# q and k projected transposed and stacked block-diagonally by DMA, four heads scored per whole-array product, in a fused attention and mixture-of-experts block

## What is computed

```python
# x [16, 256, 128]; 16 heads of 8; cos, sin [256, 4]
h = layernorm(x) * (1 + ca) + sa                 # ca, sa, ga ... per batch, from c
q, k, v = h @ WQ.T + bq, h @ WK.T + bk, h @ WV.T + bv
q, k = rope(q), rope(k)       # halves of a head: x1*cos - x2*sin, x1*sin + x2*cos
scores = einsum('bhqd,bhkd->bhqk', q, k) / sqrt(8)
attn = softmax(where(causal, scores, -inf))
x = x + ga * ((attn @ v) @ Wo.T + bo)
h = layernorm(x) * (1 + cb) + sb
x = x + gb * moe(h)           # 8 experts of 512 hidden, top 2 of 8 by the router
```

## Time and profile before

| what | value |
|---|---|
| median of 3 runs | 774.05 us (770.82 to 779.35) |
| the profiled execution | 777.98 us |
| its span, first to last instruction | 776.2 us |
| PE busy | 610.2 us (79%) |
| DVE busy | 443.2 us (57%) |
| ACT busy | 364.6 us (47%) |
| POOL busy | 355.9 us (46%) |
| mean granted TensorE clock | 0.719 |

### The profile page before, as it was taken

One profiled execution on the slowest core, in us unless ns is written; L12 is line 12 of the kernel. 1 busy time (PEld: TensorE's weight loads), 2 busy tenths in 40 slices (PEclk: granted clock), 3 DMA queues, 4 the chain that ended last, 5 costly groups with the idle time before them and its releaser, 6 DMA issues.

```text
span 776.2 us, 15198 instructions
## 1 busy us (share of the span) xinstructions
PE 610.2 (79%) x4224; PEld 450.2 (58%) x4224; DVE 443.2 (57%) x1882; ACT 364.6 (47%) x1003; POOL 355.9 (46%) x515
## 2 busy tenths in 40 slices
PE   1589898898899889888986667586698787899960
PEld 1355665565655555656554444354488677798960
DVE  2367657647465585575696838270356644467753
ACT  0234553553544535545433434243376655677740
POOL 2223344343242442442523665645335477755552
PEclk9755866755655666666565858565599999999985
DMA  3833199000000000000000000100112122233433
GB/s 100 268 114 125 42 130 126 15 8 8 7 7 14 7 7 14 5 9 7 7 15 4 26 31 18 32 18 27 28 36 55 46 74 69 73 83 99 141 87 118
DMA packets 48560, 40.70 MB, mean 52 GB/s; under 512 B 6347, under 2 KB 44756, under 8 KB 48257
## 3 DMA queue, kind: packets, MB, share of 16 engines
q1 hardware_dynamic: 43968, 31.68, 18.6%
q0 software_dynamic: 4544, 8.47, 3.3%
HBM read 24.35 MB, written 16.69 MB: 53 GB/s over the span
## 4 chain that ended last, share of the span: by engine, by line
PE 54%; DVE 15%; POOL 10%; issue 9%; DMA 7%; ACT 3%; DVEq 1%; SPq 1%; POOLq 0%; ACTq 0%
PE ps_pv L1327 9%; PE misc L1270 8%; PE ps_sc L1310 5%; PE misc L1378 5%; PE ps_max L1292 5%; DVE ps_max L1074 4%; POOL sorted_rows L537 4%; PE ps_sc L1218 4%; PE misc L1349 3%; DMA results<-qkv,probs 3%; PE ps_max L1225 2%; DMA probs<-sorted_rows 2%; PE ps_max L1294 2%; POOL probs L575 2%; PE ps_pv L1225 2%
## 5 line engine op out<-in xcount | busy, mean ns | idle before, releaser
L1074 DVE CUSTOM_DVE_ANT_0 ps_max<-ps_max,mask_q 128x128 f32<-128x128 f32 (+1 forms) x512 | 166.4, 389 | 79.2 <-PE ps_max L1294 79.0
L743 ACT ACTIVATE probs<-ps_sc 128x384 f32<-128x384 f32 x256 | 121.8, 490 | 184.3 <-PE ps_sc L1312 183.1
L575 POOL TENSOR_SCALAR_AFFINE_SELECT probs<-probs 128x512 f32<-128x512 f32 x128 | 81.8, 641 | 167.5 <-ACT probs L743 167.4
L1327 PE MATMUL ps_pv<-probs,v_wides 128*32 128x256 f32 (+1 forms) x1024 | 87.1, 483 | 29.5 <-POOL probs L575 29.4
L546 POOL DMA_INDIRECT results<-qkv,probs x78 | 79.3, 1017 | 67.6 <-DVE qkv L891 54.3
L1310 PE MATMUL ps_sc<-qm_stack,k_stacks 26*128 26x256 f32 x256 | 104.0, 480 | 2.5 <-ACT probs L743 2.5
L702 ACT ACTIVATE early_a<-ps_sc,v_wides 128x128 f32<-128x128 f32 x312 | 98.4, 373 | 3.2 <-PE ps_sc L1218 2.7
L1218 PE MATMUL ps_sc<-x_in,v_wides 128*128 128x128 f32 x624 | 87.3, 285 | 6.9 <-DVE probs L883 6.6
L1218 PEld LDWEIGHTS ps_sc<-x_in,v_wides 128*128 128x128 f32 x624 | 78.1, 197 | 10.1 <-issue 9.6
L1292 PEld LDWEIGHTS ps_max<-k_stacks,q_stack 24*128 24x128 f32 x256 | 39.0, 239 | 67.1 <-DVE maxima L1074 41.3
L1327 PEld LDWEIGHTS ps_pv<-probs,v_wides 128*32 128x32 f32 x1024 | 35.7, 147 | 68.0 <-POOL probs L575 29.4
(11 more groups left out here) (135 smaller groups left out, 1034.5 us busy)
## 6 DMA issues: line engine op xcount, KB each, us to landing
sorted_rows<-blank_s SPq DMA_DIRECT2D x1, 5070.0 KB, 42.5
probs<-sorted_rows SPq DMA_DIRECT2D x78, 65.0 KB, 1.9
gates<-gate_rows SPq DMA_DIRECT2D x1, 4096.0 KB, 12.5
x_in<-in_x SPq DMA_DIRECT2D x16, 128.0 KB, 2.1
x_res<-in_x SPq DMA_DIRECT2D x16, 128.0 KB, 2.1
wfc_s<-in_w_fc SPq DMA_DIRECT2D x1, 2048.0 KB, 9.3
wproj_s<-in_w_proj SPq DMA_DIRECT2D x1, 2048.0 KB, 8.8
heads_ts<-results SPq DMA_DIRECT2D x8, 256.0 KB, 3.1
```

The source lines that it names most:

```text
L575: nc.gpsimd.affine_select(two, two, [[0, 2], [0, 2], [1, P]], ALU.is_ge, 0.0, base=0, channel_multiplier=-1).then_inc(S["causal_done"], 1)
L743: nc.scalar.activation(probs[:, h % 8, :], ps_sc[h % 2][:, 0:384], ACT.Exp, scale=SCALE).then_inc(S["exp_done"], 1)
L1074: last = nc.vector.tensor_tensor_reduce(ps_max[h % 3][:, a * P:a * P + n], ps_max[h % 3][:, a * P:a * P + n], mask_q[:, T - n:T], 1.0, MASKED,
L1327: last = nc.tensor.matmul(ps_pv[rows, a * P:T], vw[:, a, h, :], probs[:, h % 8, :].rearrange("p (c q) -> p c q", q=P)[:, a:3:2, :], start= ...
```

## The change

A step now has 12 slots (units), three to each group of four heads: units 0 and 1 hold two heads each with queries 0 to 255 against keys 0 to 127, unit 2 holds four heads with the later queries against the later keys. A unit is 512 columns. t starts at -2.

- The weights' columns are permuted once. q and k of batch t+1 are projected transposed (`qk`, two products of 256 columns), and once more with the halves of each head exchanged (`rot`, two more); v has its own two products of 128 columns. DVE adds bias and multiplies by the cosine or sine in one instruction (4 per step), POOL sums 512 columns, ACT writes the high part, DVE the low part (one of 512 columns each), and v's bias (`values`).
- SP stacks the parts: 26 DMAs from SBUF to SBUF per step (`stack_rows`), k block-diagonally in a tensor that is zero elsewhere. It waits for the low part of batch t+1 and for the last scores of batch t-1.
- First pass: one whole-array product of 512 columns per unit, and a second product (identity by mask, both bf16) of 512 or 256 columns that adds the mask. DVE takes plain maxima, one TENSOR_REDUCE of 512 per unit.
- Shifts: per group of four heads DVE writes 16 columns (2 instructions), PE transposes them (`sh0` to `sh3`), ACT copies, SP writes them with 4 DMAs into the rows of q (`shift_rows`).
- Second pass: 2 or 4 whole-array products per unit. Unit u is scored in slot u + 7, that is from slot 7 of step t to slot 6 of step t+1 (`LAG = 7`). exp takes 512 columns, 12 times a step.
- Heads are turned back in slot 10 of step t+1, one step sooner. The gates come by one DMA per step; one for the end of the kernel is a broadcast of 2 MB in step 3, ahead of the blanking.

```diff
+UNITS = 3 * GROUPS
+LAG = 7
-    for t in range(-1, FIRST):
+    for t in range(-2, FIRST):
 USES = {
...
+    0: [('zT', 1), ('attnT', -2)],
+    1: [('sh3', -1), ('qk', 1)],
+    2: [('rot', 1)],
+    3: [('wo', -2)],
+    4: [('sh0', 0)],
+    7: [('sh1', 0), ('z2T', -2)],
+    9: [('router', -2), ('v', 1)],
+    10: [('sh2', 0), ('heads0', -1), ('heads1', -1)],
 }
+PV_AT = {11: (0, 0), 2: (1, -1), 5: (2, -1), 8: (3, -1)}
+SHIFT_AT = {2: 0, 5: 1, 8: 2, 11: 3}
+def exp_unit(n):
+    return ((n - LAG) % UNITS, -1 if n < LAG else 0)
...
+                def shift_rows(g, d):
+                    if s.has(d):
+                        s.wait(sp, S["shift_out"], d, 4, g + 1)
+                        for part in range(2):
+                            for a in range(TILES):
+                                at = (a * 2 + part) * 4
+                                sp.dma_start(part_rows(q_stack[(s.t + d) % 2], part)[:, g, a * P:(a + 1) * P],
+                                             shift_t[g % 2][at:at + 4, :].bitcast(F32)).then_inc(S["shift_in"], 16)
+                def stack_rows():
+                    if not s.has(1):
+                        return
+                    s.hold(sp, S["low_done"], 1, 1, 1, S["sp_passed"])
+                    s.hold(sp, S["score_mm"], -1, UNITS, UNITS, S["sp_passed"])
+                    n = (s.t + 1) % 2
+                    for w in range(4):
+                        for j, part in enumerate((high, low, high)):
...
+                            sp.dma_start(k_diag[n][at:at + DK, :, w, :].bitcast(F32), part[ROWS * w:ROWS * (w + 1), 1, :].bitcast(F32)).then_inc(S["stacked"], 16)
+                        for j, part in enumerate((high, high, low)):
...
+                    for part in range(2):
+                        sp.dma_start(part_rows(q_stack[n], part), zero_row[:].bitcast(F32).rearrange("p (o t) -> p o t", o=1).broadcast_to([4, GROUPS, T])
+                                     ).then_inc(S["stacked"], 16)
+                shift_rows(3, -1)
+                shift_rows(0, 0)
+                stack_rows()
+                shift_rows(1, 0)
+                shift_rows(2, 0)
...
                 if s.t == 3:
+                    sp.dma_start(gates[:], gate_dram[:, D:2 * D].rearrange("(o b) d -> o b d", o=1).broadcast_to([P, B, D])
+                                 ).then_inc(S["gate_in"], 16)
...
+                for n in range(UNITS):
...
+                    if s.has(0):
+                        maxima_of(n)
+                        if n in SHIFT_AT:
+                            shift(SHIFT_AT[n])
+                    if n == 2 and s.has(1):
+                        turn_with("qk", turned_a, 0, "qk_turned")
+                    if n == 3 and s.has(1):
+                        turn_with("rot", turned_b, 2, "rot_turned")
                     if n == RESIDUAL_AT and s.has(-2):
                         residual()
...
+                    if n == 6 and s.has(1):
+                        low_part()
...
+                def scores(u, d):
+                    g, c = divmod(u, 3)
+                    if c == 0:
+                        s.wait(pe, S["shift_in"], d, 4 * SHIFTED, SHIFTED * (g + 1))
...
+                    u, d = exp_unit(n)
+                    if s.has(d):
+                        scores(u, d)
+                    if n in PV_AT and s.has(PV_AT[n][1]):
+                        weigh(*PV_AT[n])
+                    for name, d in USES.get(n, []):
                         if s.has(d):
-                            fill(name)
+                            fill(name, d)
                     if s.has(0):
-                        for m in MAX_AT.get(h, ()):
-                            scores_for_max(m)
+                        scores_for_max(n)
```

More of the change, by code:

```diff
@@ L246, in block_program @@
         gate_row = sb("gate_row", [B, 4 * D])
-        gates = sb("gates", [P, B, 4 * D])
+        gate_now = [sb(f"gate_now{n}", [P, 4 * D]) for n in range(2)]
+        gates = sb("gates", [P, B, D])
         x_in = [sb(f"x_in{n}", [P, TILES, D]) for n in range(2)]
@@ L1047, in divide @@
+                    s.wait(dve, S["attn_tr"], -2, 1, 1)
                     nc.vector.tensor_tensor(attn[:, a], m[:, :, 0:DK],
@@ new lines, in shift @@
+                def shift(g):
+                    s.wait(dve, S["max_done"], 0, UNITS, 3 * g + 3)
+                    if g >= 2:
+                        s.hold(dve, S["shift_tr"], 0, 4, g - 1, S["dve_passed"])
+                    else:
+                        s.hold(dve, S["shift_tr"], -1, 4, g + 3, S["dve_passed"])
+                    if s.t == 0 and g == 0:
+                        dve.wait_ge(S["zeroed"], 8)
+                    m = maxima[:, :, 4 * g:4 * g + 4]
+                    v = shifts[:, g % 2, 0:16].rearrange("p (a f w) -> p a f w", a=TILES, f=2)
+                    nc.vector.tensor_scalar(v[:, :, 0], m, -1.0, None, ALU.mult).then_inc(S["shift_high"], 1)
+                    s.wait(dve, S["shift_high"], 0, 4, g + 1)
+                    nc.vector.scalar_tensor_tensor(out=v[:, :, 1], in0=m, scalar=-1.0, in1=v[:, :, 0].bitcast(F32),
+                                                   op0=ALU.mult, op1=ALU.subtract).then_inc(S["shifts_done"], 1)
@@ L1117, in emit @@
+                    if n == 8 and s.has(2):
+                        s.slot_wait(dve, x_loaded, 2)
+                        statistics(s, 2, x_in[s.t % 2], stats, moments, "stats_done", "moments_done")
+                    if s.t == LAST and 4 * n < GROUP_TILES[0]:
+                        if n == 0:
                             dve.wait_ge(S["loaded_w"], 48)
                             dve.wait_ge(S["logits_done"], GROUP_B[0])
-                        find_top(range(3 * h, min(3 * h + 3, GROUP_TILES[0])))
@@ L1144, in _ @@
+                    if n == 9 and s.has(1):
+                        values()
+                    if n == 10 and s.has(2):
+                        normalise(s, 2, x_in[s.t % 2], moments, rstd, z, "rstd_done", "z_done", "zt_done")
+                    if n == UNITS - 1 and s.has(-1):
+                        divide(0)
+                        divide(1)
             steps(dve, emit)
@@ L1315, in weigh, with shift_turned @@
+                def shift_turned(g, d):
+                    s.wait(pe, S["shifts_done"], d, 4, g + 1)
+                    bank = take(f"sh{g}", s)
+                    nc.tensor.transpose(bank[:, 0:P], shifts[:, g % 2, :].bitcast(F32), ident_s[:]).then_inc(S["shift_tr"], 1)
                 def weigh(g, d):
```

701 lines of the change are left out of this document (337 added, 364 removed), and 3 rows, old and new, of the table freed.

## The result

The changed kernel takes 1059.12 us (median of 4 runs, 1050.39 to 1059.94), the kernel before 776.33 us beside it: ratio 1.363, 95% interval 1.352 to 1.374. The prediction, 889 us with a range of 815 to 945, had the sign and the mechanism, and was 170 us short. (A slip in the text above: the broadcast of gates ahead of the blanking is 1 MB, not 2 MB.)

A forecast was written before the change was run, and what follows sets the result against it. SP's DMA queue was to bound each step at 36.4 us (22.6 + 13.8). Fill, twelve steps, blanking, routing and sorting reached 626 us, the experts 676; with 214.8 behind, span 891, execution 893, at the median 889 us; range 815 to 945.

The forecast's parts named there:

- the ring that the prediction names: Per step, 26 stacking DMAs and four with group 1's shifts hold PE, whose later slots lead to the next stacking; 36.4 us.
- S: Moment in slot 6 when DVE has written the low part and SP starts the 26 stacking DMAs.
- U: Moment at the head of slot 10 when PE goes on, group 1's shifts having landed; forecast 13.8 us after S.
- blanking, above a step: In step 3, shifts of group 3 stand behind the blanking on SP's queue and PE waits for them; 41 us.
- U(2): U of step 2, the end of the fill; forecast at 137 us.
- routing and sorting, shown: Time added to the steps: 8 us for the routing and 3 where POOL's sorting shows.
- U(14) to the experts: End of attention: 22 us for slots 11 to 6 without projection, 8 for step 15's slots 7 to 11, 20 for step 16.
- Hidden queue, faster: Rival: issues of 0.2 us or less fit inside slots 7 to 9; step some 25 us, kernel about 735; chance 0.05.
- Cold: Rival: each step begins with an idle PE, so the clock stays low; step 40.1 us, kernel 933; chance 0.17.
- Short chain: Rival: issues at 0.36 us and 19.5 us from U to S; step 32.1 us, kernel 837; chance 0.18.
- blanking harmless: Rival: small DMAs pass the blanking, so it doesn't hold the shifts; kernel 848 us; chance 0.08.
- signs of being wrong: L1382 waiting for DVE or ACT instead, a pitch far below 0.34 us, or a step below 31 us.

The follow-up runs named there:

- The experiment on shapes: The kernel before with 24 SBUF to SBUF DMAs of various shapes put on SP's queue behind the attention stage; 783.7 us in one run.
- the kernel almost without a queue: The changed kernel without 24 of its 26 stacking copies per step, scores computed from zeros; 827.3 us, ratio 1.067.
- the kernel with 807.6 us: The changed kernel with fewer stacking and shift DMAs, shifts issued by ScalarE, and cosine/sine products ahead of the maxima; 807.6 us, ratio 1.018.

## Why the prediction fell short

The structure held: the chain is the ring that the prediction names, from S through 30 issues to U and through slots 10 to 6 back to S. Its terms, measured in the round from S at 390.31 over U at 411.98 to S at 437.60:

| term | forecast | measured |
|---|---|---|
| 30 issues | 12.0 (0.40 each) | 20.6 (0.69 each) |
| from them to U | 1.8 | 1.1 |
| U to S | 22.6 | 25.6 |
| step, S to S | 36.4 | 47.3 |
| blanking, above a step | 41 | 38.4 |
| U(2) | 137 | 177.6 |
| routing and sorting, shown | 11 | 0 |
| U(14) to the experts | 50 | 52.0 |
| the rest | 214.8 | 211.9 |

**The step that failed is SP's pitch**: "bounds 0.34 and 0.47, taken 0.40, nearest to the small one with a gap". Both bounds came from transfers with one end in DRAM and were called bounds for copies within SBUF, which the trace didn't hold. The lower one was moreover how long an issue takes and not a distance from start to start. And 0.47 was not the dearest issue of that trace, which has these two as well:

```profile
34.34 0.69 SPq L439 DMA_DIRECT2D wfc_s<-in_w_fc  x1
35.07 0.66 SPq L439 DMA_DIRECT2D wfc_s<-in_b_fc  x1
```

The issues of the ring took 0.69 to 0.70, outside the range, and all 30 stand in every step. With 0.70 in the prediction's own formula S to U is 30 x 0.70 + 1.8 = 22.8, and the step 45.4. The experiment on shapes shows it by itself; leaving the copies out shows what they weigh.

**Second, U to S was forecast 3.0 us too short.** "Now DVE sets the pace" added up VectorE's instructions of slots 2 to 6 and missed that the products with the tables empty a PSUM bank that TensorE's next use of it waits for, and that they stood behind maxima of 0.69 us that nobody awaited yet. With the products moved ahead, U to S was 22.7. The forecast took the clock as warm from slot 1 on, and with that order it was 0.93; in the changed kernel it was 0.81, and in the round at 0.73 U to S took 28.6. So the handovers and the clock behind them are the miss together, and the 22.6 came out as if the other order had stood there. A maximum was taken at 0.60 and took 0.69. Slot 11 ended its first pass 4.9 to 6.0 us behind U, forecast 5.9, the 6.0 in that round at 0.73.

**The sum closes.** From U of step 2 to U of step 14 (177.62 to 792.83) are 615.2 us; the forecast's twelve steps with the blanking and 11 for routing and sorting were 489. Less the stall the twelve are 48.1 each, 11.7 above forecast: +140. The stall gives 3 back, routing and sorting hide wholly in SP's shadow and give back 11 (the steps around them are 48.2 and 47.1 us). Ahead of U(2) the fill is 40.6 us late: the first stack has landed 7 us later than forecast (54.2 for 47), and each of the three steps to U(2) is 10 to 12 us longer, as they have the same issues. 126 + 41 + 2 - 3 = 166, and 893 + 166 = 1059.

**The blanking was right in size and only half right in cause.** The forecast had TensorE going on 54 us behind U; it was 56 (226.17 to 282.23). But the prediction put it to SP's order. Issued from POOL's queue the blanking still held the shifts, not in their issue but in their landing, and in both kernels TensorE went on within 1 us of the blanking's landing; in pieces it costs a few us.

**The rivals.** *Hidden queue, faster*: refuted by the pitch, and its 25 us by the kernel almost without a queue. They were a sum of loads; at those loads the step took 33.2, and the edits to VectorE's order show that handovers fill a part of the rest. *Cold*: the steady step's clock was 0.75; no. *Short chain* and *blanking harmless*: no. None of the rivals, and none of the signs of being wrong, had a pitch above 0.47.

**Slips in the sums**, each too small to matter: the routing is 40.0 less 30.8, 9.2 and not 8; U to S at 1.2 GHz is 22.6 and 3.4, 26.0 and not 26.3; a step of 28 wants issues of 0.12 and not 0.15. And that the clock falls at an idle stretch can't be read from a window's mean of 0.61; the trace does show it by single microseconds, 1.00 until 366.7 with PE idle from 365.7 on, and 0.59 in the next.

**The clock.** PE's load was forecast as equal, its gain to come from the clock. That was about so: 24.1 us busy in a step at 0.75 for 27.4 at 0.61. In the kernels that wait less it was higher still, 0.81 with the copies left out, 0.89 in the kernel with 807.6 us, where PE was busy 74% of the step; before, it was busy 89% at 0.61. The prediction put little weight on the rule of the Trainium skill (TensorE: Matmul & The Clock Gate, Part 4: PE-mode transpose) that transposes don't lift the clock. The steps here, with 18 transposes a step in place of 38 and a warmer clock in spite of more gaps, go the page's way, while the earlier trace rows went against it. The change also replaced products of 26 rows by whole arrays, and no run tells the two apart; that stays open.

## What to carry to other kernels

Count the DMA issues that stand ahead of one that somebody waits for, and price them with a measured issue of the same kind (SBUF to SBUF, the same number of partitions); where the trace has none, the neighbours' prices are no bounds, and its dear issues (here 0.69) belong into the range. Fewer copies and a second issuing engine were worth 107 and 111 us here, more than the change saved in any engine's busy time. When such a ring is opened, look for the next one in the table of waits before you price the gain: here came first the stack, then VectorE's order, then the blanking. The remedy that was worth some 5% by itself (1059 to 1011, 852 to 808) was to let VectorE first empty the bank that TensorE awaits, and then do what nobody awaits yet.

## What the runs showed of the hardware

- An issue on SP's queue between SBUF and SBUF takes 0.50 to 0.77 us, by the number of partitions and not steadily: 8 partitions 0.65 to 0.77, 4 partitions 0.50 to 0.62, 16 partitions 0.58 to 0.61, 128 partitions 0.52 to 0.54. Gathered from four times as many partitions, in smaller pieces, 8 take 0.68 to 0.70 (flat 0.65 to 0.67) and 32 take 0.64 to 0.65 (flat 0.55).
- ScalarE issues four DMAs with shifts in 2.1 to 2.8 us, 0.5 to 0.7 each, about as SP does.
- A transfer of 5 MB on one queue holds small ones on another: issues of 0.67 us took up to 1.49, and shifts issued by 180.6 us had landed only at 202.3, with the 5 MB (202.2). The same bytes in 16 pieces (4.6 us to landing) cost the kernel before nothing (1.000, 0.997 to 1.003).
- At a granted clock of 0.93 TensorE is busy 21.0 us in one step's window, at 0.71 it is 27.5.
